# Two cross-attention layers: order of the sync queue's transfers, value shares and spread moved, six stack transfers issued by ScalarE

## The reference

```
# layer 0: queries from x, keys and values from [ctx, x] (512 keys), masked
a   = softmax(q k^T / 32 + mask) v
h   = rmsnorm(a @ out_w + out_b + x) * postnorm_w
x1  = gelu(h @ mlp_w1 + mlp_b1) @ mlp_w2 + mlp_b2 + x
# layer 1: queries from x1, keys and values from layernorm(ctx) (256 keys), masked
out = x1 + tanh(gate) * (softmax(q k^T / sqrt(32) + mask) v @ Wo.T)
```

## Time and profile before

| what | value |
|---|---|
| median of the runs | 2620.76 us |
| profiled execution, its own time | 2626.29 us |
| its span | 2624.3 us |
| PE busy | 2400.1 us, 91% |
| ACT busy | 1463.5 us, 56% |
| DVE busy | 1208.0 us, 46% |
| mean granted clock of PE | 0.954 |
| share of the chain that ended last on the sync queue's L319 | 11% |

### The profile page before, as it was taken

The page is one execution under the profiler, slowest core; times in us unless marked ns, Lnnn a source line. Parts: engine busy times, 40 slices in busy tenths (PEclk is TensorE's granted clock), DMA queues, the critical chain, the costliest instruction groups (busy, mean ns, idle before and its releaser), DMA issues. The chain is left out here.

```text
span 2624.3 us, 43886 instructions
## 1 busy us (share of the span) xinstructions
PE 2400.1 (91%) x14656; PEld 1957.9 (75%) x14656; DVE 1208.0 (46%) x2382; ACT 1463.5 (56%) x3386; POOL 231.3 (9%) x260
## 2 busy tenths in 40 slices
PE   6988888998888888988999999999989999999997
PEld 4667766776777677766888888888777788787876
DVE  4455555555444555544211221122165656666663
ACT  3666666766666666774322222222246667676766
POOL 1000000000000000001000000000032121212110
PEclk8899999999999999988999999999979899999998
DMA  6333344433443333344101110112044545445442
GB/s 172 78 85 88 93 105 105 96 89 97 105 105 97 85 87 86 90 129 141 49 1 48 48 48 2 46 48 80 11 143 106 138 106 136 124 121 139 118 126 73
DMA packets 148186, 239.00 MB, mean 91 GB/s; under 512 B 25600, under 2 KB 59680, under 8 KB 148144
## 3 DMA queue, kind: packets, MB, share of 16 engines
q1 hardware_dynamic: 148144, 238.46, 34.0%
HBM read 86.28 MB, written 25.21 MB: 42 GB/s over the span
## 5 line engine op out<-in xcount | busy, mean ns | idle before, releaser
L539 ACT ACTIVATE l_score_ps<-l_score_ps,l_neg_max 128x512 f32<-128x512 f32 (+1 forms) x1024 | 567.7, 561 | 194.5 <-DVE l_neg_max L763 192.5
L763 DVE TENSOR_REDUCE l_neg_max<-l_score_ps 128x1 f32<-128x512 f32 (+1 forms) x768 | 497.6, 683 | 106.4 <-PE l_score_ps L1045 105.8
L559 ACT ACTIVATE l_probs<-l_score_ps 128x1024 f32<-128x1024 f32 x384 | 382.9, 1019 | 177.3 <-PE l_score_ps L1078 175.6
L1045 PE MATMUL l_score_ps<-l_stack 97*128 97x512 f32 (+1 forms) x1024 | 311.5, 373 | 67.6 <-DMA l_stack<-l_qk 39.6
L1411 ACT ACTIVATE mlp_hidden<-mlp_hidden_ps,mlp_b_col 128x512 f32<-128x512 f32 x128 | 88.3, 690 | 496.3 <-PE mlp_hidden_ps L67 496.2
L1446 DVE TENSOR_TENSOR mlp_hidden_l<-mlp_hidden,mlp_hidden_h 128x512 fp32r<-128x512 f32 x128 | 94.1, 735 | 517.7 <-ACT mlp_hidden_h L1413 517.7
L1078 PE MATMUL l_score_ps<-l_stack 99*128 99x256 f32 x1536 | 258.1, 303 | 80.0 <-DMA l_stack<-l_shiftT 75.7
L1078 PEld LDWEIGHTS l_score_ps<-l_stack 99*128 99x128 f32 x1536 | 227.6, 204 | 127.3 <-issue 98.3
L1045 PEld LDWEIGHTS l_score_ps<-l_stack 97*128 97x128 f32 x1024 | 179.7, 199 | 114.6 <-ACT l_score_ps L539 79.3
L539 ACT ACTIVATION_READ_ACCUMULATOR l_score_ps<-l_score_ps,l_neg_max 128x1 f32 x1024 | 217.5, 212 | 0.0
L65 PE MATMUL mlp_hidden_ps<-mlp_norm_h,mlp_w_l 128*128 128x512 f32 x512 | 200.2, 391 | 6.4 <-DVE mlp_norm_l L1441 6.4
(11 more groups left out here) (136 smaller groups left out, 4247.4 us busy)
## 6 DMA issues: line engine op xcount, KB each, us to landing
l_stack<-room SPq DMA_DIRECT2D x256, 192.0 KB
l_stack<-l_qk SPq DMA_DIRECT2D x256, 128.0 KB
l_stack<-room SPq DMA_DIRECT2D x128, 128.0 KB
l_stack<-l_qk SPq DMA_DIRECT2D x256, 64.0 KB
l_tokens<-in_x SPq DMA_DIRECT2D x16, 512.0 KB, 4.1
l_tokens<-in_ctx SPq DMA_DIRECT2D x16, 512.0 KB, 5.5
l_stack<-room SPq DMA_DIRECT2D x128, 64.0 KB
l_rows<-in_x SPq DMA_DIRECT2D x16, 512.0 KB, 3.4
```

The lines of the kernel that those rows point to most:

```text
L539: m = act.activation(e, e, ACT.Exp, bias=neg_max[:, q, h:h + 1], accum_out=row_sum[:, q, h:h + 1])
L559: act.activation(probs[:, s % PROBS, :].rearrange("p (a b) -> p a b", a=2), score_ps[:, 2 * (s % 2):2 * (s % 2) + 2, :], ACT.Exp).then_inc ...
L763: dve.tensor_reduce(out, bank, AXIS_X, ALU.max, negate=True).then_inc(max_done, 1)
L1045: m = pe.matmul(out, stack[0:ROWS_MAX, h, P * q:P * (q + 1)], stack[0:ROWS_MAX, h, K_COLS], start=True, stop=True)
```

## The change

On SP, in both layers: the token loads come first, then the shift rows of half 0, then the residual rows, in layer 0 the norm store, and then the shift rows of half 1. On PE: `spread_sums(a, 0)` goes from the end of the last slot to behind `turn_shift(a, 1)` among the quarters of item 7, and value shares 2 and 3 stand after items 0 and 1. In layer 1, 6 of the 16 transfers of half 1 are issued by ACT at the end of its second pass.

```diff
-    SPREAD_SLOT = TURN_SLOT + 2
...
+        def move_stack(queue, half, j, slots):
+
+            def move(slot, to_cols, src):
                 heads = slice(HALF * half + j, HALF * (half + 1), HG)
+                queue.dma_start(f32(stack[DH * slot:DH * (slot + 1), heads, to_cols]), f32(src)
+                                ).then_inc(stack_loaded[half], 16)
+            src = qk[DH * j:DH * (j + 1), GROUPS * half:GROUPS * (half + 1), :]
+            if 0 in slots:
+                move(0, Q_COLS, src[:, :, Q_HIGH])
+                move(0, K_COLS, src[:, :, K_HIGH])
+            if 1 in slots:
+                move(1, slice(0, WIDTH), src[:, :, 0:WIDTH])
+            if 2 in slots:
+                move(2, slice(0, WIDTH), src[:, :, WIDTH:2 * WIDTH])
...
+        SLOTS_OF_ACT = {} if first else {HG - 2: (1, 2), HG - 1: (0, 1, 2)}
...
+        def slots_of_sp(half, j):
+
+            behind = SLOTS_OF_ACT.get(j, ()) if half == HALVES - 1 else ()
+            return tuple(slot for slot in range(SPLIT) if slot not in behind)
...
-                if first and a is not None:
+                if p is not None and not (isinstance(p, int) and p == B - 1):
+
+                    sp.wait_ge(item_done, ITEMS * p + NT)
+                    load_tokens(sp, p + 1)
...
+                if a is not None:
+                    load_shift(0)
                     load_rows()
                 if first and prev is not None:
                     sp.wait_ge(nT_done, prev + 1)
                     sp.dma_start(result[prev], nT[:, :, :]).then_inc(stored, 16)
-                if p is not None and not (isinstance(p, int) and p == B - 1):
-
-                    sp.wait_ge(item_done, ITEMS * p + NT)
-                    load_tokens(sp, p + 1)
-                if not first and a is not None:
-                    load_rows()
                 if a is not None:
...
+                    load_shift(1)
...
                 exps(a, 7)
                 o_high(a, 2)
                 o_high(a, 3)
+                if p is not None:
+                    act.wait_ge(shifted_done, PSTEPS * (a + 1))
+                    act.wait_ge(low_done, ITEMS * (p + 1))
+                    for j, slots in SLOTS_OF_ACT.items():
+                        move_stack(act, HALVES - 1, j, slots)
...
-                    if a is not None and SLOT[slot][0] == "item" and 1 <= n < FB - 1:
-                        v_share(a, n + 1)
+                    if a is not None and SLOT[slot][0] == "item" and n < FB - 2:
+                        v_share(a, n + 2)
...
-                    if a is not None and SPREAD_SLOT == slot:
-                        spread_sums(a, 0)
...
                     if q == 2:
                         turn_shift(a, 1)
+                        spread_sums(a, 0)
```

More of the change, by code:

```diff
@@ L313, in load_tokens, with load_stacks @@
             sp.dma_start(tokens[:, QT:2 * QT, :], c_view[b]).then_inc(tokens_loaded, 16)
-        def load_stacks(sp, b, half, lows):
-            def move(slot, j, to_cols, src):
+        def move_stack(queue, half, j, slots):
+            def move(slot, to_cols, src):
                 heads = slice(HALF * half + j, HALF * (half + 1), HG)
-                sp.dma_start(f32(stack[DH * slot:DH * (slot + 1), heads, to_cols]), f32(src)
-                             ).then_inc(stack_loaded[half], 16)
+                queue.dma_start(f32(stack[DH * slot:DH * (slot + 1), heads, to_cols]), f32(src)
[8 more added lines that the diff above has]
+                move(2, slice(0, WIDTH), src[:, :, WIDTH:2 * WIDTH])
+        def load_stacks(sp, b, half, lows, slots_of):
             sp.dma_start(f32(stack[MASK_ROW:MASK_ROW + 1, HALF * half:HALF * (half + 1), K_COLS]),
@@ L325, in load_stacks, with every_slot @@
             for j in range(HG):
[L326 to L330, removed]
+                move_stack(sp, half, j, slots_of(half, j))
+        SLOTS_OF_ACT = {} if first else {HG - 2: (1, 2), HG - 1: (0, 1, 2)}
+        def every_slot(half, j):
+            return tuple(range(SPLIT))
+        def slots_of_sp(half, j):
+            behind = SLOTS_OF_ACT.get(j, ()) if half == HALVES - 1 else ()
+            return tuple(slot for slot in range(SPLIT) if slot not in behind)
         block = ctx.enter_context(nc.Block())
@@ L366, in load_rows, with load_shift @@
                     sp.dma_start(rows[:, :, :], res_view[a]).then_inc(rows_loaded, 16)
-                if first and a is not None:
+                if p is not None and not (isinstance(p, int) and p == B - 1):
+                    sp.wait_ge(item_done, ITEMS * p + NT)
+                    load_tokens(sp, p + 1)
+                def load_shift(half):
+                    sp.wait_ge(shift_copied, HALVES * a + half + 1)
+                    for part in range(2):
+                        sp.dma_start(
+                            f32(stack[SHIFT_ROW + part:SHIFT_ROW + part + 1,
+                                      HALF * half:HALF * (half + 1), Q_COLS]),
+                            f32(shiftT[HALF * part:HALF * (part + 1), half:half + 1, :]),
+                        ).then_inc(shift_loaded[half], 16)
+                if a is not None:
+                    load_shift(0)
                     load_rows()
@@ L372, in iteration @@
                     sp.dma_start(result[prev], nT[:, :, :]).then_inc(stored, 16)
-                if p is not None and not (isinstance(p, int) and p == B - 1):
-                    sp.wait_ge(item_done, ITEMS * p + NT)
-                    load_tokens(sp, p + 1)
-                if not first and a is not None:
-                    load_rows()
-                if a is not None:
[L380 to L387, removed]
+                if a is not None:
+                    load_shift(1)
                 if p is None and load_ahead is not None:
@@ L400, in iteration @@
                         load_stacks(sp, p, half, ITEMS * p + NT + NK + half + 1 if first
-                                    else ITEMS * p + NT + GROUPS * (half + 1))
+                                    else ITEMS * p + NT + GROUPS * (half + 1),
+                                    every_slot if a is None else slots_of_sp)
                 if a is not None and not first:
```

## The result

The changed kernel takes 2507.4 us (median of 4 runs, 2504.85 to 2508.12), against 2620.4 of the kernel before beside it: ratio 0.957, interval 0.9555 to 0.9588. That is 113 us less. The forecast was 2495 with a range of 2475 to 2522, so the time lies in the range, 12 above the forecast. The profiled execution took 2504.85, with a span of 2502.7.

The account below looks back on a forecast made before the run. PE's waits for late shift rows and the norm (layer 0) and half 1's stack (layer 1) were read first. Gains 115.0 + 5 + 5.6 = 125.6 off 2626.3 give 2500.7; less 5.5 for the median, 2495; range 2475 to 2522.

Parts of the forecast that it names:

- Shift rows first, with the spread: Layer 0: shift rows arrive before PE wants them and the norm wait goes; 8.5 us an iteration, 115.0 in all.
- Rival 4: Layer 0: the shift rows stay late, 1.95 of wait in each iteration; 27 us more, 2522; chance 0.08.
- the 14th iteration: Layer 0 iteration without a token load in front: waits 1.95, keeps its clock; forecast gain 2.1 us.
- Spread behind the second turn: Layer 0: takes PE off the norm wait, counted with the shift rows; layer 1: 0, at most 4 us either way.
- Shares in layer 0: Earlier value shares fill PE's wait of 0.4 for the value copy: -5 us, bounds -6 and 0.
- Shares in layer 1: Item 2's transposes come later, ACT idles 1.2 us, value copies end later: period 1.05 us longer.
- Six transfers on ACT: Layer 1: six issues, 3.8 us, hide in ACT's 5.12 idle; stack wait goes, worth almost nothing in a quiet iteration.
- Rival 1: Layer 1: the two queues take turns issuing, ACT's six last 7.7 us; 22 more, 2517; chance 0.15.
- Rival 2: Layer 1: earlier shares cost nothing, period 41.06, 14.6 us less: 2480; chance 0.12.
- rival 3: Layer 1: the whole stack wait comes back, period 38.7, 48 us less: 2447; chance 0.05.
- Rival 5: Layer 1: an issue on ACT blocks it; 2570 at 1.94 us, slower than before above 2.55; chance 0.05.
- Layer 1 in sum: Layer 1: fourteen periods of 42.1, gain 2.6 us, and 3 in the last iteration: -5.6.

Follow-up runs that it names:

- number 6: Kernel before with only the new sync queue order and the moved spread (old share places, all transfers on SP): 2510.5 us, ratio 0.9573.
- Number 10: Changed kernel with the token loads back behind the norm store, only the shift of half 1 behind them: 2509.9 us, ratio 0.9567.
- number 9: Kernel before with new sync order and moved spread, but half 0's shift rows behind residual rows and norm store: 2581.0 us, ratio 0.9852.
- Number 8: Changed kernel with the spread of half 0 back at the end of the last slot: 2514.4 us, ratio 0.959.
- number 7: Changed kernel with layer 1's value shares in their old places and no transfers on ScalarE: 2505.1 us, ratio 0.955.
- number 2: Changed kernel, but in layer 1 only value share 2 stands early, share 3 back behind item 2: 2487.5 us, ratio 0.9493.
- numbers 1 and 4: The first: changed kernel with layer 1's old share places, 2487.6 us; the second: kernel before with only ScalarE's six transfers of half 1, 2606.0 us.

## Why the prediction was right, and where it was off

- *Shift rows first, with the spread (110.5 + 2.1 + 2.4 = 115).* Right in mechanism and size. The period fell from 71.7 to 63.34 by this part alone (number 6), 8.4 where 8.5 was worked out, and layer 1's first POOL instruction comes 113.9 earlier, where 115.0 was. The layout gave a new wait for the last sum and it is there, 0.72. Number 10 adds what the prediction had not separated: it is enough to move the first shift rows ahead of the store that waits for DVE; the tokens have no part once they stand in front. Behind the store the token loads did cost: with them and the spread moved and the shift rows still there (number 9) the period is 68.2.
- *Rival 4, the shift rows still late.* It did not happen, but its price was wrong. The prediction took the 14th iteration's 1.95 and a full clock, and by its term of 1.2 the norm's wait with it: 3.15 a period, a gain of 6.4 and 2522. Number 9 shows what the same order costs when the spread has also moved: a gain of 3.5 a period, 2581. The wait is not far off, 3.90. The step that failed is the full clock: before, the two waits of 1.21 and 1.95 stood apart, with a quarter of item 7 between them; in one piece they are followed by a clock of 0.50, which loses 1.7 to 2.5 us a period. With the 0.75 of longer wait that is the 2.9 between 6.4 and 3.5. The upper end of the range was 60 us too low for this case.
- *Spread behind the second turn.* Number 8: worth 0.33 a period, where a reader of the earlier trace rows would book 1.2.
- *Shares in layer 0 (-5).* The size came out, by luck in good part: 5.0 by the traces and 5.5 by the medians of numbers 6 and 7. The reason given, a wait of 0.4 filled in each steady iteration, gives only 0.12 a period, 1.8 in fourteen. The wait for the value copies is gone, but others for DVE's `hT` copies take most of its place. The rest came in the first and the last iteration, which the prediction had not counted.
- *Shares in layer 1 (+1.05 a period).* Right, to the instruction: ACT idles 1.20 where 1.2 was worked out, and the value copies come 1.25 later (number 2). The cost is 1.28 in a steady period and 20.9 in fourteen, as four periods of the changed kernel are 43 and more; 14.7 had been worked out. Three of those have no larger wait of PE than their neighbours but a mean clock of 0.92 (number 7), the fourth has the one stack wait, 0.95. That the longer waits for ACT would cost clock is what the prediction left out.
- *Six transfers on ACT.* Right: 3.8 us hidden in 5.12, measured 3.96 in the iteration shown and 4.72 at most. Rival 1, that the queues take turns for a whole issue, falls by the rows: 0.66 an issue on ACT while the sync queue keeps 0.65. By the rule of the Trainium skill that was weighed there (Perfetto Trace Analysis, section on the HWDGE DMA instruction: a shared descriptor generator, the lock wait inside the duration) one of the two should have lasted longer; this trace does not bear that out for a whole issue. A lock held for a small part of one is not excluded: the sync queue's overlapping issues last 0.645 on average, the others 0.613.
- *The other rivals.* Rival 2 (earlier shares cost nothing) and rival 3 (the whole stack wait comes back, a period of 38.7) fall with numbers 1 and 4: without the new shares and without the stack wait the period is 41.1, the 41.06 of the quiet iteration of before. Rival 5 would have needed 2.55 us an issue on ACT; the longest of the changed kernel lasted 0.957.
- *Layer 1 in sum (-5.6).* Measured 2.5, and luck is in it. The period was to be 42.1 and is 42.3, and the sum 596.3 where 589.4 was forecast: the fourteen periods lost 4.3 where 2.6 were to be gained. Against that, the first period is 4.7 shorter in this execution. In every other version it takes 49.6 to 51.1, with both edits of layer 1 too (50.0 and 49.7), so the 47.3 is no effect of the edits.

The 12 us between forecast and median come from three places. The forecast took 5.5 off for the profiled execution of before being above its median; that of after is 2.6 below its own. Against its own execution the forecast was 2500.7, and 2504.85 came: 4 us, 3 of them in layer 1.

## What to carry to other kernels

On an in-order queue, look for the short transfer that stands behind a command that waits for another engine, and move that one; its neighbours' places may be worth nothing (number 10). Price a rival with the whole change in place: a wait read from the old trace may have had another wait spent in front of it. Read the granted clock by period: two periods with the same instructions differed by 1.5 us through it (41.06 and 42.54), and a mean over the layer hides that. And two edits whose gain and loss meet on one path are to be run each alone: here one was worth 17 us and the other cost 12 or more, the pair was worth nothing, and leaving the shares of layer 1 where they stood gives 2487.5, 0.8% under the changed kernel.

## What the runs showed of the hardware

- Two queues issued stack transfers at once, each at nearly its own pace: 0.66 and 0.65 us an issue in the iteration shown, against 0.64 for the sync queue alone.
- The time from the issue of the first shift rows to PE's start on them differed with what stood ahead of them: 2.82 us behind a norm store only (number 9), 4.97 with both token loads just ahead (666.06 to 671.03).
- In layer 0 gaps of 3.90 and 3.92 us on PE were followed by a granted clock of 0.50 (5.0 us of it, and a mean of 0.66 over 5 us), where a gap of 1.95 was followed by none. In layer 1 the length of one gap does not tell: before, stack waits of 2.2 to 2.4 were followed by the full clock in six periods and by a stretch at 0.50 in five, and in the changed kernel the clock fell in ten periods without any single wait above 0.97.
